# A graph attention kernel on one core: the transpose of the cross scores goes from a TensorE product to copies, block moves and 32 by 32 transposes

## The reference, cut to what matters

```python
u = einsum('bid,bjd->bij', h, h) / sqrt(384)      # 64 x 64 scores of each graph
a = softmax(u); delta = a * adj
attn = delta / (delta.sum(-1) + 1e-10)
hl, hs, hr = h @ Wl.T + bl, h @ Ws.T + bs, h @ Wr.T + br
ctx = (attn * upper) @ hl + diag(attn) * hs + (attn * lower) @ hr
out = relu(layernorm(ctx) * g + beta)
# before the first and the third layer: h = relu(layernorm(x))
```

## Time and profile before

| what | value |
|---|---|
| median of 3 runs | 1219.35 us (1218.94 to 1219.39) |
| the profiled execution's own time | 1218.43 us |
| its span, first to last instruction | 1216.6 us |
| PE busy | 1201.8 us, 99% of the span |
| PEld busy | 1196.1 us, 98% |
| DVE busy | 1059.6 us, 87% |
| ACT busy | 983.2 us, 81% |
| POOL busy | 312.5 us, 26% |
| mean granted TensorE clock | 0.997 of full speed |

### The profile page before, as it was taken

The page is one execution under the profiler, slowest core; times in us unless marked ns, Lnnn a source line. Parts: engine busy times, 40 slices in busy tenths (PEclk is TensorE's granted clock), DMA queues, the critical chain, the costliest instruction groups (busy, mean ns, idle before and its releaser), DMA issues.

```text
span 1216.6 us, 26372 instructions
## 1 busy us (share of the span) xinstructions
PE 1201.8 (99%) x7071; PEld 1196.1 (98%) x7071; DVE 1059.6 (87%) x2863; ACT 983.2 (81%) x2673; POOL 312.5 (26%) x421
## 2 busy tenths in 40 slices
PE   7999999999999999999999999999999999999997
PEld 6999999999999999999999999999999999999997
DVE  6888898889887888888888888998989898998976
ACT  6777778778777788888888888888888888888874
POOL 2223232322222121212212121223333332323221
PEclk9999999999999999999999999999999999999999
DMA  5434343333232333333333323322232323322321
GB/s 181 130 115 125 100 126 100 121 94 119 85 108 72 96 101 119 93 129 107 111 116 105 110 89 109 104 86 96 98 108 97 108 97 101 102 94 97 100 92 55
DMA packets 112992, 127.63 MB, mean 105 GB/s; under 512 B 11136, under 2 KB 100224, under 8 KB 112896
## 3 DMA queue, kind: packets, MB, share of 16 engines
q1 hardware_dynamic: 112896, 126.50, 32.9%
HBM read 76.91 MB, written 49.55 MB: 104 GB/s over the span
## 4 chain that ended last, share of the span: by engine, by line
PE 95%; DVE 2%; DMA 2%; issue 1%; SPq 0%; ACT 0%; POOL 0%; POOLq 0%; DVEq 0%; ACTq 0%
PE left_bank L479 24%; PE right_bank L479 24%; PE context_bank L479 24%; PE context_bank L513 17%; PE score_bank L455 5%; DMA rows<-x 1%; PE edge_bank L463 0%; DMA squares<-turned 0%; DVE turned L860 0%; DVE in_stats L843 0%; DVE side_parts L963 0%; DVE node_t L864 0%; PE edge_bank L469 0%; DVE context L1008 0%; SPq L368 0%
## 5 line engine op out<-in xcount | busy, mean ns | idle before, releaser
L479 PE MATMUL left_bank<-weight,node_t 128*128 128x384 f32 x1728 | 338.6, 339 | 0.0
L479 PE MATMUL right_bank<-weight,node_t 128*128 128x384 f32 x1728 | 333.4, 337 | 0.0
L479 PE MATMUL context_bank<-weight,node_t 128*128 128x384 f32 x1728 | 331.0, 336 | 0.1
L479 PEld LDWEIGHTS left_bank<-weight,node_t 128*128 128x128 f32 x1728 | 304.7, 189 | 0.1
L479 PEld LDWEIGHTS context_bank<-weight,node_t 128*128 128x128 f32 x1728 | 302.3, 188 | 0.7 <-ACT context_bank L674 0.7
L479 PEld LDWEIGHTS right_bank<-weight,node_t 128*128 128x128 f32 x1728 | 298.7, 188 | 0.0
L513 PE MATMUL context_bank<-side_parts,attn_t 128*128 128x386 f32 x1152 | 239.5, 343 | 1.1 <-issue 1.1
L513 PEld LDWEIGHTS context_bank<-side_parts,attn_t 128*128 128x128 f32 x1152 | 199.8, 189 | 2.2 <-issue 1.5
L664 ACT ACTIVATE side_parts<-right_bank 128x384 fp32r<-128x384 f32 x192 | 94.5, 492 | 127.0 <-PE context_bank L513 127.0
L1223 POOL TENSOR_TENSOR rstd<-spread,scalars 128x2 f32<-128x2 f32 x95 | 68.4, 720 | 492.5 <-DVE spread L986 492.3
L680 ACT ACTIVATE context_bank<-context_bank,diag 128x386 f32<-128x386 f32 x192 | 106.7, 556 | 57.3 <-PE context_bank L479 49.9
(11 more groups left out here) (88 smaller groups left out, 1590.1 us busy)
## 6 DMA issues: line engine op xcount, KB each, us to landing
squares<-turned SPq DMA_DIRECT2D x94, 384.0 KB, 2.7
nodes<-squares SPq DMA_DIRECT2D x376, 96.0 KB, 2.2
rows<-x SPq DMA_DIRECT2D x63, 384.0 KB, 4.0
out<-rows SPq DMA_DIRECT2D x31, 384.0 KB, 2.6
adj_in<-adj SPq DMA_DIRECT2D x96, 64.0 KB, 1.9
piece<-weights SPq DMA_DIRECT2D x18, 192.0 KB, 2.5
rows<-weights SPq DMA_DIRECT2D x2, 576.0 KB, 8.1
vector_rows<-vectors SPq DMA_DIRECT2D x3, 384.0 KB, 4.2
```

Of the source, the lines that this page charges most:

```text
L479: mm = nc.tensor.matmul(bank[:, 0:D], node_t[:, s.parity, k, c, a], weight[:, s.phase % 2, w, c, b], start=False, stop=(c, a) == (CH - 1, ...
```

## The change

In phases 0 and 2, from step 3 on, `turn_cross` is not issued. The turned cross scores are made in four parts instead:

- ScalarE copies the cross scores twice, each time as two instructions of 64 partitions: once to `cross[:, 0]` (the untouched copy for `sum_scores`) and once to `cross[:, 1]`. The old second pair copied 64 x 64 elements each, the new one copies 64 x 2 x 64.
- GpSimd (`move_blocks`) overwrites the off-diagonal 32 by 32 blocks in `cross[:, 1]`: four products by one, [32, 2, 32] each, read from one quarter of the partitions and written to its neighbour. Each waits for the one before.
- VectorE (`turn_blocks`) transposes all 32 by 32 blocks of `cross[:, 1]` in one instruction, to `own_edge`.
- `add_cross` adds `own_edge` from SBUF instead of the PSUM bank.

In phase 0 VectorE's `turn_blocks` stands after the input's statistics and ahead of `norm(prev, 0)`, and GpSimd's moves stand after `output_rstd(prev)`. In phase 2 `gather_input(fourth)` is moved from behind `spreads` to ahead of `turn_blocks`, and GpSimd's moves stand ahead of `output_rstd(prev)`. Phase 1 keeps the product. The core of the diff:

```diff
+FIRST_BY_BLOCKS = 3
+
+def by_blocks(s):
+    return s.bounded and not (isinstance(s.n, int) and s.n < FIRST_BY_BLOCKS)
...
+        cross_flat = cross[:, 0].rearrange("p (k j) -> p k j", k=2)
+        cross_moved = cross[:, 1].rearrange("p (k b j) -> p k b j", k=2, b=2)
+        cross_diagonal = cross[:, 1].rearrange("p (k j) -> p k j", k=2)
+        turned_blocks = own_edge[:, :, :].rearrange("p k j -> p (k j)")
...
-                if nxt.exists():
+                if nxt.exists() and not by_blocks(nxt):
                     turn_cross(nxt)
...
             def copy_cross(s):
                 act.wait_ge(scored, s.n + 1)
-                at_least(act, cross_turned, s.n)
                 at_least(act, score_summed, 2 * s.n)
+                if by_blocks(s):
+                    act.wait_ge(cross_added, s.n)
+                    for copied in (cross_flat, cross_diagonal):
+                        for half in HALVES:
+                            nc.scalar.activation(copied[half], scores4[half, :, 1, half], ACT.Copy).then_inc(cross_packed, 1)
+                    return
...
+            def turn_blocks(s):
+
+                dve.wait_ge(blocks_moved, QUARTERS * (block_index(s) + 1))
+                nc.vector.transpose(turned_blocks, cross[:, 1].bitcast(F32)).then_inc(blocks_turned, 1)
+
             def add_cross(s):
 
-                dve.wait_ge(cross_turned, s.n + 1)
                 dve.wait_ge(score_summed, 2 * s.n + 2)
+                if by_blocks(s):
+                    dve.wait_ge(blocks_turned, block_index(s) + 1)
+                    nc.vector.tensor_tensor(score[:, :, :], score[:, :, :], own_edge[:, :, :], ALU.add).then_inc(cross_added, 1)
+                    return
+                dve.wait_ge(cross_turned, turn_index(s) + 1)
                 nc.vector.tensor_tensor(score[:, :, :], score[:, :, :], turned_cross, ALU.add).then_inc(cross_added, 1)
...
+                if nxt.exists() and by_blocks(nxt) and s.phase < 2:
+                    turn_blocks(nxt)
                 if prev.exists() and not prev.level():
                     norm(prev, 0)
+                if nxt.exists() and by_blocks(nxt) and s.phase == 2:
+                    if fourth.exists():
+                        gather_input(fourth, 0)
+                        gather_input(fourth, 1)
+                    turn_blocks(nxt)
                 if nxt.exists():
                     add_cross(nxt)
...
-                if s.phase != 1 and fourth.exists() and fourth.bounded:
+                if s.phase == 0 and fourth.exists() and fourth.bounded:
                     gather_input(fourth, 0)
                     gather_input(fourth, 1)
...
+            def move_blocks(s):
+
+                pool.wait_ge(cross_packed, 4 * (s.n + 1))
+                if s.phase == 0:
+                    pool.wait_ge(rstd_done, s.n - 1)
+                else:
+                    pool.wait_ge(blocks_placed, s.n)
+                copied = cross_flat.rearrange("p k (b j) -> p k b j", b=2).bitcast(F32)
+                for q in range(QUARTERS):
+                    r, here, other = q % 2, q * Q, (q ^ 1) * Q
+                    at_least(pool, blocks_moved, QUARTERS * block_index(s) + q)
+                    ones = vector_rows[other:other + Q, 0, 5 * D:5 * D + 1].unsqueeze(2).to_broadcast([Q, 2, Q])
+                    block = copied[other:other + Q, :, r]
+                    nc.gpsimd.tensor_tensor(cross_moved[here:here + Q, :, 1 - r], block, ones, ALU.mult).then_inc(blocks_moved, 1)
...
+                if nxt.exists() and by_blocks(nxt) and nxt.phase == 2:
+                    move_blocks(nxt)
+                    pool.wait_ge(blocks_moved, QUARTERS * (block_index(nxt) + 1))
                 if prev.exists():
                     output_rstd(prev)
+                if nxt.exists() and by_blocks(nxt) and nxt.phase == 0:
+                    move_blocks(nxt)
+                    pool.wait_ge(blocks_moved, QUARTERS * (block_index(nxt) + 1))
```

More of the change, by code:

```diff
@@ L96, in slot, with block_index, turn_index @@
         return bass.ds(2 * self.g + k, 1)
+FIRST_BY_BLOCKS = 3
+def by_blocks(s):
+    return s.bounded and not (isinstance(s.n, int) and s.n < FIRST_BY_BLOCKS)
+def block_index(s):
+    return s.normal - FIRST_BY_BLOCKS
+def turn_index(s):
+    return s.n if s.phase == 0 else s.n - PAIRS + FIRST_BY_BLOCKS
 def at_least(eng, sem, value):
@@ L264, in adj_gnn_program @@
         cross_turned = sem("cross_turned")
+        blocks_moved = sem("blocks_moved")
+        blocks_turned = sem("blocks_turned")
         cross_added = sem("cross_added")
@@ L614, in copy_cross @@
                 act.wait_ge(scored, s.n + 1)
-                at_least(act, cross_turned, s.n)
                 at_least(act, score_summed, 2 * s.n)
+                if by_blocks(s):
[4 more added lines that the diff above has]
+                    return
+                if s.phase == 1:
+                    act.wait_ge(cross_added, s.n)
+                else:
+                    at_least(act, cross_turned, s.n)
                 for h, half in enumerate(HALVES):
@@ L878, in sum_scores @@
                 for h, half in enumerate(HALVES):
-                    nc.vector.tensor_tensor(score[half], scores4[half, :, 0, half], cross_here[h].bitcast(F32),
+                    copied = cross_flat[half] if by_blocks(s) else cross_here[h]
+                    nc.vector.tensor_tensor(score[half], scores4[half, :, 0, half], copied.bitcast(F32),
                                             ALU.add).then_inc(score_summed, 1)
+            def turn_blocks(s):
+                dve.wait_ge(blocks_moved, QUARTERS * (block_index(s) + 1))
+                nc.vector.transpose(turned_blocks, cross[:, 1].bitcast(F32)).then_inc(blocks_turned, 1)
             def add_cross(s):
-                dve.wait_ge(cross_turned, s.n + 1)
                 dve.wait_ge(score_summed, 2 * s.n + 2)
+                if by_blocks(s):
[3 more added lines that the diff above has]
+                dve.wait_ge(cross_turned, turn_index(s) + 1)
                 nc.vector.tensor_tensor(score[:, :, :], score[:, :, :], turned_cross, ALU.add).then_inc(cross_added, 1)
```

## The result

The changed kernel takes 1253.72 us (1253.02 to 1254.68), the one before 1219.37. The ratio is 1.0285, with a 95% interval of 1.0273 to 1.0297: slower, inside the predicted range of 1228 to 1265, and 8.7 us above the predicted 1245. The profiled execution took 1254.3 us, its span is 1252.5.

A forecast was written before the change was run, and what follows sets the result against it. TensorE's gapless chain was taken as the bound, to be replaced in phase 2 by a loop through ScalarE, GpSimd and VectorE: 1218.4 - 2.5 + 28.8 = 1244.7, forecast as 1245 us, range 1228 to 1265.

The forecast's parts named there:

- The predicted ladder: Phase 2, from one LEFT half of the weigh product to the next: pieces in sequence summing to 13.24 us against 12.34.
- TensorE's 0.9 us: Phase 2: idle time on TensorE ahead of the weigh product's LEFT half, released by VectorE's last split.
- the step of phase 2: Each of 32 steps was to take 13.24 us instead of 12.34, losing 0.90: +28.8 us.
- The line between 2 and 128 elements: GpSimd's block moves: 0.197 us at 2 elements a partition, 0.465 at 128, so 0.33 at 64.
- the bounds of 1.04 and 2.10 us: Four block moves with wakes: lowest at 0.20 us each, highest at 0.465 each; the forecast took 1.57.
- Rival A: Block moves cheap, 1.04 us at a fixed price each: phase 2 +11.8, phase 0 -3.2, median 1228 us; chance 0.10.
- rival B: Block moves dear, 2.10 us or more: phase 2 +45.8, phase 0 +6.5, median 1272 us; chance 0.10.
- The floor: Phase 2, VectorE's own shorter loop: 12.62 us a step even if the moves cost nothing.
- can't shrink: Phase 2: the 5.05 us from `spreads` to the last split stay, as `norm(prev, 0)` waits for GpSimd's `rstd`.
- The saved product: TensorE's chain: 0.15 us less a step without the turning product, 9.2 us over 61 steps if nothing else waits.
- Phase 0: Nine steps with a weight piece lose 0.06 us each, 20 others save 0.15 each: -2.5 us in all.
- rival C: TensorE keeps its pace at 12.20 us a step in phase 2, with L864 shortened: 1210 us; chance 0.05.

The follow-up runs named there:

- run 1: The changed kernel with all 32 steps of phase 2 written out, no loop: 1241.14 us, ratio 1.0183 against the kernel before.
- run 2: The kernel before, turning product kept, with all steps of phase 2 written out: 1218.42 us, ratio 0.9998.
- run 7: The changed kernel with the block moves left out, so the turned scores hold wrong off-diagonal blocks: 1230.32 us, ratio 1.0096 against the kernel before.
- run 5: The changed kernel with `spreads` ahead of the transpose in phase 2 and all of phase 2 written out: 1214.96 us, ratio 0.9967 against the kernel before.

## Why the prediction was right, and where it was off

**The mechanism held.** A loop through ScalarE, GpSimd and VectorE took TensorE's place as the bound of phase 2. The predicted ladder beside the one measured in a written-out step (run 1) and in a step of the changed kernel's loop, in us. The step of run 1 is the one from 1024.42 to 1037.59.

| piece | predicted | written out | in the loop |
|---|---|---|---|
| LEFT half to the end of the copies | 5.81 | 5.82 | 5.96 |
| GpSimd wakes | 0.08 | 0.08 | 0.24 |
| four moves | 1.57 | 1.38 | 1.39 |
| VectorE wakes | 0.04 | 0.03 | 0.03 |
| transpose to addition | 0.36 | 0.42 | 0.42 |
| addition to spread | 0.29 | 0.21 | 0.21 |
| spread to the end of the last split | 5.05 | 5.08 | 5.27 |
| TensorE wakes | 0.04 | 0.15 | 0.14 |
| sum | 13.24 | 13.17 | 13.66 |

That the sum comes so near for a written-out step is in part luck: the moves and the way from addition to `spread` were priced 0.19 and 0.08 us too high, TensorE's start and the way from transpose to addition 0.11 and 0.06 too low. The first row agrees by luck too. TensorE took 0.08 us more from the LEFT half to `scores` (3.75 against 3.66, as the half that had waited takes 0.77 us where the RIGHT half takes 0.69), and ScalarE ended its copies 0.08 sooner behind `scores` (2.07 against 2.15). The waits were foreseen as such, with other sizes: TensorE's 0.9 us was 0.69 written out and 1.06 to 1.19 in the loop, VectorE's 0.7 ahead of the transpose 0.43 and 0.60, and its 0.8 ahead of the norm 0.87 and 0.91.

**The term that was mis-sized is the step of phase 2, at 0.90 us lost "in each of the 32 steps".** The written-out steps lost 0.74 to 0.83 each. The 26 in the loop lost 1.25 on average, 32.6 us in all against 23.4 for that number of steps. The prediction read every piece from a loop step of the kernel before, where register instructions are issued while the engine still works on something else, and took it that they stay hidden. The runs show that the loop's form costs 0.43 us a step once the chain runs through the other engines: run 1 put the steps at 13.17, and run 2 showed that the kernel before pays nothing for its loop. That it is the register instructions, one after the other where their engine waits, is the reading that fits and is not shown by itself. By intervals, the difference of 9.6 us between the predicted 1244.7 and the profiled 1254.3 is made of this +9.2, -0.6 for the five steps written out (3.9 against 4.5, the last one from the end of the span), -1.0 for step 63, which I priced at 0.9 and which lost nothing, +0.2 in phase 1, +0.5 in phase 0 and +1.3 at the start.

**The moves:** 0.288 us each against 0.33, started 0.37 apart against 0.41. The rows for one move and one transpose in phase 2:

```profile
L1292 POOL TENSOR_TENSOR cross<-cross,vector_rows x100: 283/288/293, 861.7 to 1189.2; 32x64 fp32r<-32x64 f32 x100
...
L919 DVE STREAM_TRANSPOSE own_edge<-cross x25: 311/311/315, 863.1 to 1189.5; 128x128 f32<-128x128 f32 x25
```

The line between 2 and 128 elements was nearly right, and the bounds of 1.04 and 2.10 us held it. Rival A (all of a move's cost is fixed) and rival B (dear, or held up by VectorE) both fell. Rival A's sum has a slip of its own: it puts phase 0 at -3.2 us, but by the prediction's own times the statistics let the transpose start no earlier there than in the forecast (275.65 against 275.64), so phase 0 should stand at -2.5.

**The floor:** VectorE's own loop "even if the moves cost nothing" was put at 12.62; run 7 gave 12.55 written out, and it was still slower than before, as said. But it is a floor of this order of the queue only, and not of VectorE's work: the 5.05 us behind `spreads`, of which the prediction says that it "can't shrink", hold the wait for `rstd`. With `spreads` ahead of the transpose the steps took 12.29 us with all four moves (run 5).

**The saved product:** 0.13 us where it stood between others, against 0.15 predicted. The weigh product and the turning product gave their 0.07 and 0.06; the 0.02 on the right product were not there. That is nearer to the chain's 0.15 than to the 0.081 from the Trainium skill's page "TensorE: Matmul & The Clock Gate", section "Back-to-back issue gap"; the rows decide.

**Phase 0:** 12.41 predicted and measured in the steps with a weight piece, but of other parts, so this agreement is luck. The norm came 0.33 us late and not 0.48: the statistics alone set the transpose (without the moves, in run 7, these steps take as long), where the prediction had moves and statistics end together. And the stall cost TensorE about 0.2 us behind the low part, 0.15 to start and some 0.08 more inside the LEFT half, not 0.04.

**Faster (rival C)** would have needed the two loops to shorten, and I gave it 0.05 by way of L864. That mechanism fell: the row is L897 now, 1.79 us in phase 2, beside 1.83 before. But faster than before was not out of reach: run 5 shortened the ladder by another way, the order of `spreads` in VectorE's queue, and phase 2 came to 12.29 us. The rival's own 12.20 us a step and 1210 us no run reached; the best is 1214.88.

## What to carry to other kernels

Work that is taken off the busiest engine must be followed round the whole loop to where that engine waits next: 0.13 us saved a step cost 1.25 here, because copies, moves, transpose, addition and a round trip to GpSimd stood one behind the other in front of the last low part. When a wait is put into a queue, look at once at what behind it another engine is waiting for, and move that ahead; one line was worth 26 us. And the loop's form was free here only while TensorE was the bound: once the chain runs through the other engines' queues, write the steps out, or count on a cost like the 0.4 us a step here.

## What the runs showed of the hardware that was not expected

- GpSimd's instructions of 32 x 64 elements start 0.37 us apart though each lasts 0.288, and waiting for the one before adds nothing to speak of (four of them: 1.37 us without the waits, 1.39 with them).
- Released by VectorE between the halves of the weigh product, TensorE starts 0.14 to 0.15 us behind the end of VectorE's instruction (1037.44 to 1037.59), more than VectorE takes to start its transpose behind GpSimd (0.03). The three products that had waited take 0.77 us, the three ahead of them 0.69.
- A short stall inside a group of products shows in no idle time: the group of six has 1.27 or 1.42 us instead of 1.21.
